# The prologue of a one-core MoE layer pair, reordered: constants first, blocks spread by scalars, second-layer loads moved into the loop

## The reference, cut to what matters

```python
x = x + attn(layernorm(x))      # gate_w routes; softmax weights of the two best
x = x + ffn(layernorm(x))       # router_w routes; sigmoid weights, gated FFN per expert
...
def _expert(x, ...):            # of the first layer
    xn = _layernorm(x, ln_w)
    up = xn @ w_up;  x_m, z = up[:, :I], up[:, I:]
    conv = x_m * conv_w[:, -1] + conv_b;  conv_act = silu(conv)
    q, k, v = headwise(conv_act, q_w), headwise(conv_act, k_w), headwise(x_m, v_w)   # 4x4 blocks
    ig = concat([q, k, v]) @ ig_w + ig_b
    h = (qk / (max(|qk|, exp(-ig)) + 1e-6)) * vh;  hn = normalised per head
    return x + ((hn * on_w + skip_w * conv_act) * silu(z)) @ w_down
```

## Time and profile before

| | us |
|---|---|
| timed, median of 3 | 379.27 |
| timed, lowest and highest | 376.4, 379.41 |
| span of the profiled execution | 411.5 |
| the profiled execution's own time | not given by the page beside its span |
| busy in the span: PE, DVE, ACT, POOL | 316.7, 261.2, 168.6, 213.0 |

### The profile page before, as it was taken

One profiled execution on the slowest core, in us unless ns is written; L12 is line 12 of the kernel. 1 busy time (PEld: TensorE's weight loads), 2 busy tenths in 40 slices (PEclk: granted clock), 3 DMA queues, 4 the chain that ended last, 5 costly groups with the idle time before them and its releaser, 6 DMA issues.

```text
span 411.5 us, 6611 instructions
## 1 busy us (share of the span) xinstructions
PE 316.7 (77%) x1789; PEld 239.2 (58%) x1789; DVE 261.2 (63%) x876; ACT 168.6 (41%) x482; POOL 213.0 (52%) x242
## 2 busy tenths in 40 slices
PE   0929998899898888888788597868048979999920
PEld 0819865688677776777677443425025546666610
DVE  4866982796787677776888729385027456544406
ACT  2705943645354545454456204411002115566610
POOL 4998635367676666655674414237740001656530
PEclk9999999999999999999999789999659989999985
DMA  4499966024223332233354050001121000322125
GB/s 129 165 310 252 88 180 221 15 106 142 103 93 133 126 104 90 105 142 100 114 168 143 14 206 10 2 13 54 55 65 47 0 0 14 84 76 75 45 87 200
DMA packets 32883, 41.97 MB, mean 102 GB/s; under 512 B 9040, under 2 KB 24080, under 8 KB 32720
## 3 DMA queue, kind: packets, MB, share of 16 engines
q1 hardware_dynamic: 28400, 32.59, 26.9%
q0 software_dynamic: 4256, 8.74, 7.3%
q10 hardware_dynamic: 192, 0.23, 0.2%
HBM read 15.90 MB, written 10.32 MB: 64 GB/s over the span
## 4 chain that ended last, share of the span: by engine, by line
PE 28%; issue 25%; DVE 19%; POOL 17%; DMA 4%; another core or an unknown queue 3%; ACT 2%; POOLq 0%; DVEq 0%; ACTq 0%; SPq 0%
PE psum L987 8%; POOL yrows L651 7%; POOL xslots L645 6%; PE psum L1034 4%; PE psum L1007 3%; PE psum L966 2%; PE psum L1012 2%; DVE x L1402 2%; PE psum L1028 2%; DMA blocks<-yrows 2%; POOL headsum L530 2%; DVE onehot L1267 1%; PE psum L1044 1%; DVE wraw L1391 1%
## 5 line engine op out<-in xcount | busy, mean ns | idle before, releaser
L651 POOL DMA_INDIRECT yrows<-yx,blocks x31 | 29.7, 958 | 63.0 <-ACT yx L831 56.3
L620 POOL TENSOR_TENSOR rh<-c2ve,neghalf 128x8 f32<-128x8 f32 (+1 forms) x23 | 34.1, 1483 | 44.3 <-DVE c2ve L1378 41.4
L1070 PE MATMUL psum<-x1T,rec 128*128 128x512 f32 x64 | 33.2, 647 | 23.2 <-issue 17.0
L595 POOL DMA_INDIRECT xg<-xrows,gidx x39 | 39.9, 1022 | 19.2 <-issue 11.0
L606 POOL DMA_INDIRECT yrows<-yx,sidx x39 | 39.4, 1010 | 12.5 <-issue 8.6
L987 PE MATMUL psum<-yx,blocks 128*128 128x256 f32 (+1 forms) x184 | 43.4, 358 | 0.5 <-issue 0.5
L987 PE MATMUL psum<-wraw,blocks 128*128 128x256 f32 (+1 forms) x92 | 22.4, 365 | 16.6 <-DVE wraw L1391 15.0
L1070 PEld LDWEIGHTS psum<-x1T,rec 128*128 128x128 f32 x64 | 11.5, 198 | 37.5 <-issue 27.5
L805 ACT ACTIVATE xn<-psum 128x512 f32<-128x512 f32 x16 | 9.3, 596 | 55.9 <-PE psum L1070 41.8
L1114 PE MATMUL psum<-rec,yx 128*128 x62 | 31.9, 596 | 0.0
L987 PEld LDWEIGHTS psum<-yx,blocks 128*128 128x128 f32 x184 | 29.2, 191 | 2.4 <-issue 0.7
(11 more groups left out here) (221 smaller groups left out, 832.6 us busy)
## 6 DMA issues: line engine op xcount, KB each, us to landing
blocks<-rec SPq DMA_DIRECT2D x23, 523.0 KB
blocks<-yrows SPq DMA_DIRECT2D x7, 512.0 KB, 5.0
blocks<-wd SPq DMA_DIRECT2D x23, 128.0 KB
wraw<-in_L_attn_w_up SPq DMA_DIRECT2D x1, 2048.0 KB, 18.2
blocks<-xslots SPq DMA_DIRECT2D x31, 64.5 KB, 2.4
xslots<-zrow SPq DMA_DIRECT2D x1, 1984.0 KB, 19.3
x<-in_L_attn_hidden_states SPq DMA_DIRECT2D x4, 256.0 KB, 5.3
rec<-in_L_ffn_w_gate SPq DMA_DIRECT2D x1, 1024.0 KB, 17.1
```

The lines of the kernel that those rows point to most:

```text
L595: g.indirect_dma_start(xg[:, b, h, :], None, xrows, bass.IndirectOffsetOnAxis(ap=gidx[0][:, unit(j) + h:unit(j) + h + 1], axis=0)).then_in ...
L620: g.tensor_tensor(rh[:, 0:n], c2ve[:, 0:n], neghalf[:, 0:n * NH].rearrange("p (h k) -> p h k", h=n), ALU.pow).then_inc(s_rh, 1)
L651: g.indirect_dma_start(yrows[1], bass.IndirectOffsetOnAxis(ap=xin2[:, j % R2I, D:D + 1].bitcast(U32), axis=0), yb2[:, j % R2Y, :], None).t ...
L1070: ins = t.matmul(GUd[p][g], rec2[:, e, col + c * P:col + (c + 1) * P], x1T[:, 0:DN, :].rearrange("p i t -> p (i t)"), start=True, stop=True)
```

## The change

POOL makes its constants ahead of the norms. DVE instead of ACT norms quarters 2 and 3 of the first norm. DVE spreads the blocks by 32 tensor_scalars, one for each column block, each multiplying all 48 blocks by one column of the mask; `qkvT` changes its layout for that. `cig` goes: PE multiplies v by `centre` and by the gate columns in separate matmuls. POOL does all of the second norm (`xn`). `w_up` comes in four DMAs with a semaphore each, `ig_b` behind them into a tile of its own that ACT copies into the records. The second layer's down weights and both fills of `xslots` move from the prologue to a point of SP's loop, after the loads of tile 3's record and tile 2's `w_down`. PE's order: `prepare2(0)` ahead of the rank, experts 6 and 7 behind the permutation.

```diff
-        qkvT = sb("qkvT", [P, QB, 64])
+        qkvT = sb("qkvT", [P, 64, QB])
...
-        cig = sb("cig", [P, 2, CH, P + NH])
+        igb = sb("igb", [P, E, NH])
...
@@ block.sync
-            sp.dma_start(rec[:, :, IB:IB + NH], ig_b.unsqueeze(0).to_broadcast([P, E, NH])).then_inc(s_ib, 16)
-            sp.dma_start(wraw[:], w_up.rearrange("e d n -> d e n")).then_inc(s_wraw, 16)
+            for c in range(4):
+                es = slice(c * E // 4, (c + 1) * E // 4)
+                sp.dma_start(wraw[:, es, :], w_up.rearrange("e d n -> d e n")[:, es, :]).then_inc(s_wraw[c], 16)
+            sp.dma_start(igb[:], ig_b.unsqueeze(0).to_broadcast([P, E, NH])).then_inc(s_ib, 16)
 
             sp.wait_ge(s_raw, 16 * 10)
-            sp.dma_start(wd1[:], w_down.rearrange("e (c p) d -> p e c d", p=P)).then_inc(s_late, 16)
+            sp.dma_start(wd1[:], w_down.rearrange("e (c p) d -> p e c d", p=P)).then_inc(s_wd, 16)
...
-            for c in range(CH):
-                sp.dma_start(rec2[:, :, DOWN + c * D:DOWN + (c + 1) * D],
-                             f_down.rearrange("e (c p) d -> p e c d", p=P)[:, :, c, :]).then_inc(s_late, 16)
-            sp.wait_ge(s_fid, 2)
-            xsv = xslots.rearrange("(j p) d -> p j d", p=P)
-            sp.dma_start(xsv[:, :, 0:D], zrow[:].unsqueeze(1).to_broadcast([P, N2, D])).then_inc(s_fill, 16)
-            sp.dma_start(xsv[:, :, D:D + 1].bitcast(U32), fid[:].unsqueeze(2), allow_slow_non_contiguous=True).then_inc(s_fill, 16)
...
+            def load_second_layer():
+
+                for c in range(CH):
+                    sp.dma_start(rec2[:, :, DOWN + c * D:DOWN + (c + 1) * D],
+                                 f_down.rearrange("e (c p) d -> p e c d", p=P)[:, :, c, :]).then_inc(s_late, 16)
+                sp.wait_ge(s_fid, 2)
+                xsv = xslots.rearrange("(j p) d -> p j d", p=P)
+                sp.dma_start(xsv[:, :, 0:D], zrow[:].unsqueeze(1).to_broadcast([P, N2, D])).then_inc(s_fill, 16)
+                sp.dma_start(xsv[:, :, D:D + 1].bitcast(U32), fid[:].unsqueeze(2), allow_slow_non_contiguous=True).then_inc(s_fill, 16)
+
             for j in range(NT + 1):
                 load1(j)
                 load_down(j - 1)
+                if j == RB - 1:
+                    load_second_layer()
...
-        def spread_blocks(m):
-            n = E * CH
-            nc.vector.tensor_tensor(
-                blocks[:, m * n:(m + 1) * n, 0:P].rearrange("p m (n b) -> p m n b", b=QB),
-                blockmask[:][:, None, :, None].to_broadcast([P, n, NB, QB]),
-                qkvT[:, :, m * n:(m + 1) * n].rearrange("p b m -> p m b").unsqueeze(2).to_broadcast([P, n, NB, QB]),
-                ALU.mult).then_inc(s_blk[m], 1)
...
+        def spread_blocks():
+            m = 3 * E * CH
+            for n in range(NB):
+                nc.vector.tensor_scalar(blocks[:, :, n * QB:(n + 1) * QB], qkvT[:, 0:m, :], blockmask[:, n:n + 1], None, ALU.mult)
+            nc.vector.tensor_copy(blocks[:, 0:E * CH, P:].rearrange("p (e c) h -> p e c h", c=CH),
+                                  igT[:].rearrange("p h (e s) -> p e s h", e=E)[:, :, CH:2 * CH, :]).then_inc(s_blk, 1)
...
@@ block.gpsimd
-            def norms(k, cols, sem_out):
...
-            for p in range(2):
-                g.tensor_copy(cig[:, p, 0, 0:P], centre[:])
-                g.tensor_copy(cig[:, p, 1, NH:], centre[:])
             small = dict(allow_small_or_imprecise_dtypes=True)
             done(g.iota(ekey[:], pattern=[[-1, E]], base=E, channel_multiplier=0, **small))
...
+            def norms(k, cols, sem_out):
...
             def fold(e):
+                if e % 2 == 0:
+                    pool.wait_ge(s_wraw[e // 2], 16)
                 w = parT[:, at + e:at + e + 1]
                 g.tensor_scalar(wraw[:, e, 0:I], wraw[:, e, 0:I], w, None, ALU.mult).then_inc(s_wl, 1)
-                if e >= 2:
-                    pool.wait_ge(s_pV, e - 1)
-                g.tensor_copy(cig[:, e % 2].rearrange("p c n -> p (c n)")[:, P:P + CH * NH].rearrange("p (c h) -> p c h", c=CH),
-                              igT[:, :, 6 * e + 2 * CH:6 * e + 3 * CH].rearrange("p h c -> p c h")).then_inc(s_cig, 1)
...
             for e in range(2, E):
                 fold(e)
-                renormed(e - 2)
-            for i in range(E - 2, TT // 2):
-                ins = renormed(i)
+                for i in range(3 * (e - 2), min(3 * (e - 1), TT)):
+                    ins = renormed(i)
             ins.then_inc(s_xn, 1)
...
@@ block.scalar
-            transposed(0, 0)
-            for c in range(2, 4):
-                normed(0, x, c)
-                transposed(0, c - 1)
-            transposed(0, 3)
+            for q in range(4):
+                transposed(0, q)
...
+            a.activation(rec[:, :, IB:IB + NH], igb[:], ACT.Copy).then_inc(s_par2, 1)
...
-                if 2 <= e < 6:
-                    act.wait_ge(s_rstdn, 1)
-                    for i in range(TT // 2 + 2 * (e - 2), TT // 2 + 2 * (e - 1)):
-                        ins = a.activation(xn[:, i, :], x[:, i, :], ACT.Identity, bias=shift[:, 1, i:i + 1], scale=rstd[:, 1, i:i + 1])
...
@@ block.tensor
-                pe.wait_ge(s_cig, e + 1)
                 for c in range(CH):
                     o = c * (P + NH)
-                    ins = t.matmul(bank[1][:, o:o + P + NH], blocks[:, 2 * r + e * CH + c, 0:P], cig[:, e % 2, c, :], start=True, stop=True)
+                    v = blocks[:, 2 * r + e * CH + c, 0:P]
+                    at, ig = (o, o + P) if c == 0 else (o + NH, o)
+                    t.matmul(bank[1][:, at:at + P], v, centre[:], start=True, stop=True, skip_group_check=True)
+                    ins = t.matmul(bank[1][:, ig:ig + NH], v, igT[:, :, 6 * e + 2 * CH + c], start=True, stop=True, skip_group_check=True)
...
             prepare1(0)
             prepare1(1)
+            prepare2(0)
             route_rank(0)
-            prepare2(0)
-            for e in range(2, 7):
+            for e in range(2, 6):
...
             route_perm(0)
-            for e in range(7, E):
+            for e in range(6, E):
...
-            pe.wait_ge(s_late, 80)
+            pe.wait_ge(s_wd, 16)
...
@@ block.vector
+            for c in range(2, 4):
+                dve.wait_ge(s_rstd[0], c + 1)
+                for i in range(c * TT // 4, (c + 1) * TT // 4):
+                    ins = v.tensor_scalar(x1[:, i, 0:D], x[:, i, :], rstd[:, 0, i:i + 1], shift[:, 0, i:i + 1], ALU.mult, ALU.add)
+                ins.then_inc(s_x1v, 1)
             dve.wait_ge(s_parT, 1)
-            for m in (2, 0, 1):
-                spread_blocks(m)
+            spread_blocks()
```

More of the change, by code:

```diff
@@ L234, in program @@
         s_x = [sem(f"x_loaded{c}") for c in range(4)]
-        s_raw, s_gate, s_wraw, s_ib, s_late = (sem(n) for n in (
-            "raw_loaded", "gate_loaded", "wup_loaded", "igb_loaded", "late_loaded"))
+        s_raw, s_gate, s_ib, s_wd, s_late = (sem(n) for n in (
+            "raw_loaded", "gate_loaded", "igb_loaded", "wdown_loaded", "late_loaded"))
+        s_wraw = [sem(f"wup_loaded{c}") for c in range(4)]
         s_pool = sem("pool_step")
@@ L516, in _ @@
             select(blockmask[:], [[QB, NB]], QB - 1, -1)
+            small = dict(allow_small_or_imprecise_dtypes=True)
+            done(g.iota(ekey[:], pattern=[[-1, E]], base=E, channel_multiplier=0, **small))
+            done(g.memset(lower[:], 1.0))
+            select(lower[:], [[1, P]], -1, -1)
+            g.memset(ones[:], 1.0)
+            done(g.memset(upto[:], 1.0))
+            select(upto[:], [[1, E], [-1, E]], 0, 0)
+            g.iota(tilecut[:], pattern=[[P, NTOK // P]], base=0, channel_multiplier=0, **small)
+            g.iota(tileno[:], pattern=[[1, LNT[1] + 1]], base=0, channel_multiplier=0, **small)
+            g.iota(iota_p[:], pattern=[[1, P]], base=0, channel_multiplier=0, **small)
+            g.iota(iota_a[:], pattern=[[1, NA]], base=0, channel_multiplier=0, **small)
+            g.iota(part[:], pattern=[[0, 1]], base=0, channel_multiplier=1, **small)
+            g.iota(pairno[:], pattern=[[1, TT * TOPK]], base=0, channel_multiplier=0, **small)
+            g.iota(spare[:], pattern=[[P, NA]], base=PAIRS, channel_multiplier=1, **small)
+            g.memset(cmpj[:], 0.0).then_inc(s_const, 1)
+            g.iota(fid[:], pattern=[[P, N2]], base=PAIRS, channel_multiplier=1).then_inc(s_fid, 1)
+            for k in range(TOPK):
+                g.iota(pid[:, k, :], pattern=[[TOPK, TT]], base=k, channel_multiplier=TOPK * TT).then_inc(s_id1, 1)
             def norms(k, cols, sem_out):
@@ L533, in _ @@
             done(g.tensor_tensor(centre[:], centre[:], ident[:], ALU.add))
-            for p in range(2):
-                g.tensor_copy(cig[:, p, 0, 0:P], centre[:])
-                g.tensor_copy(cig[:, p, 1, NH:], centre[:])
-            small = dict(allow_small_or_imprecise_dtypes=True)
-            done(g.iota(ekey[:], pattern=[[-1, E]], base=E, channel_multiplier=0, **small))
```

(28 more changed lines are left out.)

36 lines of the change are left out of this document (16 added, 20 removed).

## The result

The kernel after took 390.84 us (median of four executions, 387.35 to 396.06), the kernel before beside it 379.34: 1.031 of before, 95% interval 1.022 to 1.039. The forecast of 379.8 was wrong, and the time lies outside its range (373.5 to 387.5). Ratios here leave out executions more than 1.5% above a kernel's fastest, and the profile that follows is of such a one, the slowest of the four (396.06).

What follows compares the result with a forecast made beforehand. The prediction took the prologue to be bound by POOL's late order and, behind it, DVE's spread. A loop start 2.2 us earlier and a 2.7 us wait at tile 4 summed to +0.5, so 379.8 us, range 373.5 to 387.5.

Steps and rivals of the forecast that it cites:

- Constants at no cost: Prologue: 3.1 us of POOL work goes ahead of the norms, into time in which POOL waits, and costs nothing.
- the spread's 9.1 us: DVE's prologue spread of the blocks: 32 tensor_scalars at 0.285 us each take 9.1 us, against 10.9 before.
- PE's first matmul on the blocks: Prologue: it moves from 31.08 to 23.1 us, 8.0 earlier.
- The permutation's end: End of PE's prologue routing: from 53.77 to 48.5 us, 5.3 earlier.
- the sum of +0.5 us: Whole kernel: loop start 2.2 us earlier plus a 2.7 us wait for tile 4's record, giving 379.8.
- Experts 6 and 7 behind the permutation: End of prologue: 2.4 us more PE work plus 0.7 for small matmuls, leaving 2.2 of the 5.3 us gain.
- The forecast's own sign of being wrong: First loop's start: the forecast is wrong if it comes more than 6 us earlier or at all later.
- the fills' wait: Loop, tile 4: its record queues behind the moved fills, so PE waits 2.7 us (bounds nothing to 10.5).
- the 1.7 that I added for the gathers: Landing of tile 4's record in the loop: 1.7 us more for gathers sharing the DMA engines.
- rival 2: PE's projection of tile 4: the fills hold its record, a wait of 10.5 us, 387.6 in all; chance 0.15.
- Rival 3: Prologue spread: DVE and POOL take turns for whole instructions, some 14 us more, 394; chance 0.06.
- Rival 1: Prologue's gain arrives whole: spread 3.8 us earlier at the one-hot's pace, fills land in time, 373.3; chance 0.26.

Runs made afterwards that it cites:

- a0: The kernel after again, no edit, in another job: 377.1 us, 0.999 of before.
- a1: The kernel after again, no edit, in a further job: 379.4 us, 1.002 of before.
- a2: The kernel after again, no edit, in a fourth job: 380.9 us, 1.004 of before.
- p1 to p3: Three more profiled executions of after with four idle matmuls in the permutation, one ahead of each group of eight: 382.3, 380.9 and 383.0 us.
- e1: After, with the second layer's down weights and the two fills back ahead of the row store: 378.9 us, 1.001 of before.
- e6: After, with PE's order of before and the fills back ahead of the row store: 370.8 us, 0.984 of before.
- e8 to e10: After, fills back ahead of the row store, plus: PE's order of before (371.3 us); rank ahead of expert 0's second step (372.5); expert 6 ahead of the permutation (372.0).
- e3: After, with all eight experts' records ahead of the permutation: 375.7 us, 0.995 of before.

## Why the prediction was wrong

**Right, by its steps.** Constants at no cost; the spread's 9.1 us (9.2); PE's first matmul on the blocks (22.70 for 23.1). The permutation's end (48.44 for 48.5) agrees in part by luck: the last two groups run 0.6 us longer than the first two, and in a0 it comes at 47.91. Where the clock stays, the rest holds too: clock matmuls at 55.04 (forecast 55.6), loop at 61.15 (61.8), 2.5 us earlier than in the second profile of before (forecast 2.2). The record of tile 4 comes 2.10 us late in the measured kernel, for 2.7 forecast, and 0.28 to 0.93 in the three jobs after it. That those three come near the sum of +0.5 us (0.999, 1.002 and 1.004) is luck: none of them has its two terms. Loop start, and the steps of tiles 4 and 5 beyond 7.1 each, stand at -2.5 and +0.8 in a0, +0.3 and +0.2 in a1, +0.5 and +1.2 in a2.

**The step that failed** is "Experts 6 and 7 behind the permutation", with the sentence ahead of it, that PE waits there for the one-hots. I priced that wait at its length, and the work behind it at the pace of the fast row (0.28 in the earlier trace rows). The wait comes in four short pieces with small matmuls between, and the clock went to half behind it: 10.1 us for two experts, and the loop 5.8 us later than in a0. The forecast's own sign of being wrong, a loop that starts later at all, came true. The half clock had no term in the sum. From the fast pace I had taken that PE stays fast; the earlier trace rows holds both paces, and I read the slow one as a matter of the early start alone.

**The second term** that was mis-sized is the fills' wait. The queue was right: the record comes behind the id fill's landing. The length, 2.10 for 2.7, agrees with some luck, as no run shows the 1.7 that I added for the gathers, and with a faster fill the wait was under 1.2. The price was wrong: behind 2.1 us of waiting came some 7 us at half clock, so that the steps of tiles 4 and 5 cost 5.2 us more than 7.1 each (11.2 + 8.2 - 14.2). That is rival 2's place, PE's projection of tile 4, at a lower price than its 10.5; the longer transfer that it named makes only the wait, and the clock the rest.

**How the 11.5 us come about.** The two terms, +3.2 where I had -2.2 at the loop's start (66.92 against 63.68) and +5.2 where I had +2.7, make 8.4 us in the profiled execution. That one is 20.4 above before's second profile by its span, and the other 12 lie behind the loop, most of them in the stretch at half clock. The 11.5 are of the median, and the other three executions have only their spans and clocks (385.6 to 389.2 us at 0.922 to 0.938, against 373.9 at 0.958 in a0): by the estimate above it is clock that they lost, but how it divides among the three places is not shown. Why all four executions lost so much and none of the next three jobs did so throughout stays open. The job of p1 to p3, whose before was as slow as the one beside the first measurement (380.2 and 379.3), had the slow fill and the long waits for tile 4 in all of its profiles, and after itself was not run in it.

**Rival 3** has fallen. A spread instruction takes 0.288 us (9.23 over 32) beside POOL's folds and norms, the 0.285 that I took from a row without them. By the Trainium skill (SBUF — State Buffer, Who interferes with whom) the two engines would have taken turns for whole instructions if VectorE ran this form in a two-port mode. The trace shows no such turns for it; whether it ran in that mode, no run tells. **Rival 1** would have needed a faster spread.

## What to carry to other kernels

A wait of PE has two prices: its length, and the work behind it at half clock if the clock goes. Where a trace shows PE picking at its input in pieces, put dense work ahead of it, so that it arrives when the input is complete: here one expert more ahead of the permutation, or the rank ahead of one small step, gave 1.1 to 1.2% that the 8 us of earlier blocks had not given alone. And look at the spread of the times, not only at the median: the kernel after and e1, whose executions lie 6 to 10 us apart, lost the clock in some of them; those of e6 and e8 to e10, four each, lie 1.5 to 3 us apart.

## What the runs showed of the hardware

- The same matmuls in the same order kept the granted clock at 1.00 in three profiles (waits of 2.5 to 3.0 us in the permutation) and had it at 0.50 for 7 to 14 us in four (2.0 to 2.3 us). The Trainium skill (TensorE: Matmul & The Clock Gate, Part 1: The HAM clock gate) says that the gate follows how busy the engine has been and that its moment differs from run to run of one kernel; these profiles agree.
- From 22 to 30 us of after the granted clock reads 1.00 and yet the four-column matmul takes 0.43 us, as later at 0.50 (0.28 from 33 us on). The length of a known form told more there than the clock's row.
- A load's issue on SP, mostly 0.49 us elsewhere in the loop, lasted 3.9 to 6.4 us behind the id fill (15.5 KB in four-byte pieces, 19 to 22 us to landing). In e3, where SP came to it 21.7 us after the loop's start instead of 19.1, it took 0.50 us. With the fills back ahead of the row store, that store's issue took 3.6 to 6.0 us behind the id fill, 0.35 without.
- One execution of before had a span 37.6 us longer than the next (411.5 and 373.9), with eight steps of its loop at 8.5 to 8.6 us instead of 7.1, at a granted clock of 1.00. A second profile of the kernel before would have told this before the forecast was made.
